# Two attention and mixture-of-experts layers: in an expert step, both transposes between gate/up and the down product

## The reference

```
x = x + L0_xattn(norm(x), ctx)          # 16 heads of 16 channels, cross attention
x = x + L0_ffn(norm(x))                 # 16 experts, 4 a token, chosen by groups; a shared expert
x = x + L1_xattn(norm(x), ctx, mask)    # the same with biases and a mask
x = x + L1_ffn(norm(x))                 # 16 experts, 2 a token; a shared expert
```

## Time and profile before

| what | value |
|---|---|
| time, median of 3 (lowest, highest) | 2484.33 us (2482.01, 2484.53) |
| the profiled execution's own time | 2487.88 us |
| its span | 2486.0 us |
| TensorE busy, matmuls | 2044.5 us (82%) |
| TensorE busy, weight loads | 1599.3 us (64%) |
| VectorE, ScalarE, GpSimd busy | 59%, 43%, 45% |
| granted TensorE clock, mean | 0.931 |
| expert phases | about 774 to 1257 us and 2041 to 2287 us |

### The profile page before, as it was taken

The page is one execution under the profiler, slowest core; times in us unless marked ns, Lnnn a source line. Parts: engine busy times, 40 slices in busy tenths (PEclk is TensorE's granted clock), DMA queues, the critical chain, the costliest instruction groups (busy, mean ns, idle before and its releaser), DMA issues.

```text
span 2486.0 us, 52846 instructions
## 1 busy us (share of the span) xinstructions
PE 2044.5 (82%) x16352; PEld 1599.3 (64%) x16353; DVE 1467.8 (59%) x4591; ACT 1068.5 (43%) x2276; POOL 1121.9 (45%) x1595
## 2 busy tenths in 40 slices
PE   4999999999965999999948989889998849997000
PEld 3777777777754878777736766666666637786000
DVE  3677777777762444444436877777777624443333
ACT  2555555555522333333325555555555513332000
POOL 1455555555556000000056777777777341001676
PEclk8999999999987999999969999999999969999555
DMA  5222222222226444444434333333333154444555
GB/s 204 58 79 80 79 80 80 82 82 78 76 83 148 150 146 150 151 146 151 149 123 171 102 101 101 103 101 107 98 102 101 41 105 150 150 149 132 177 175 169
DMA packets 206442, 292.77 MB, mean 118 GB/s; under 512 B 34230, under 2 KB 155320, under 8 KB 205880
## 3 DMA queue, kind: packets, MB, share of 16 engines
q1 hardware_dynamic: 164199, 185.12, 22.9%
q0 software_dynamic: 37584, 102.81, 13.2%
q10 hardware_dynamic: 4608, 4.20, 1.3%
HBM read 155.69 MB, written 136.33 MB: 117 GB/s over the span
## 4 chain that ended last, share of the span: by engine, by line
PE 59%; POOL 18%; issue 12%; DVE 4%; DMA 4%; ACT 2%; SPq 1%; POOLq 1%; DVEq 0%; ACTq 0%
PE ps L1435 16%; POOL ygath L615 10%; PE ps L1443 7%; PE ps L1371 5%; POOL xsort L559 4%; PE ps L1448 4%; PE ps L1309 3%; PE ps L1287 3%; PE ps L1321 3%; PE ps L1263 3%; PE ps L1346 2%; PE ps L1380 2%; PE ps L1454 2%; POOL rstd L631 2%; PE ps L1230 2%
## 5 line engine op out<-in xcount | busy, mean ns | idle before, releaser
L1435 PE MATMUL ps<-wgu,ygath 128*128 x1664 | 441.3, 388 | 27.6 <-issue 23.0
L559 POOL DMA_INDIRECT xsort<-xn,xidx x384 | 386.7, 1007 | 134.7 <-issue 133.4
L615 POOL DMA_INDIRECT ygath<-ysort,yidx x384 | 372.5, 970 | 152.1 <-issue 99.1
L928 DVE TENSOR_REDUCE mx<-ps 128x16 f32<-128x1920 f32 x128 | 276.2, 2158 | 191.1 <-PE ps L1287 190.8
L1175 DVE TENSOR_TENSOR ygath<-ygath,ps 128x128 f32<-128x128 f32 x416 | 119.7, 288 | 442.8 <-ACT ygath L842 442.8
L1435 PEld LDWEIGHTS ps<-wgu,ygath 128*128 128x128 f32 x1664 | 285.3, 191 | 73.8 <-issue 51.6
L607 POOL CAST yidx<-rows_of 128x8 uint32 (+1 forms) x64 | 12.9, 201 | 682.2 <-SPq L297 680.4
L1371 PE MATMUL ps<-W,wsgu 128*128 128x256 f32 x1024 | 253.3, 391 | 13.7 <-ACT rt L789 12.9
L846 ACT ACTIVATE ygath<-ps 128x256 f32<-128x256 f32 x416 | 159.8, 384 | 231.4 <-PE ps L1448 231.2
L1443 PE MATMUL ps<-wd,ygath 128*128 x832 | 248.1, 380 | 2.8 <-DVE ygath L1187 2.8
L842 ACT ACTIVATE ygath<-ps 128x128 f32<-128x128 f32 x416 | 115.5, 278 | 301.4 <-PE ps L1435 301.3
(11 more groups left out here) (174 smaller groups left out, 3836.2 us busy)
## 6 DMA issues: line engine op xcount, KB each, us to landing
ygath<-xsort SPq DMA_DIRECT2D x416, 128.0 KB, 2.1
ysort<-ygath SPq DMA_DIRECT2D x208, 256.0 KB, 2.3
based<-XO SPq DMA_DIRECT2D x64, 256.0 KB, 2.3
XB<-in_x SPq DMA_DIRECT2D x32, 256.0 KB
wgu<-in_wgu SPq DMA_DIRECT2D x2, 4096.0 KB, 13.7
XB<-based SPq DMA_DIRECT2D x32, 256.0 KB
X<-based SPq DMA_DIRECT2D x32, 256.0 KB
out_x<-X SPq DMA_DIRECT2D x32, 256.0 KB, 2.3
```

Of the source, the lines that this page charges most:

```text
L559: e.indirect_dma_start(out=xsort, in_=xn2[s][:, t, :], in_offset=None, out_offset=bass.IndirectOffsetOnAxis(ap=xidx[s][:, t * 4 + k:t * 4 ...
L615: e.indirect_dma_start(out=ygath[s][:, t * 4 + k, :], out_offset=None, in_=ysort, in_offset=bass.IndirectOffsetOnAxis(ap=yidx[s][:, t * 4 ...
L928: e.tensor_reduce(mx[:, r].rearrange("p j t h -> p j (t h)"), ps[:, 4 * s:4 * s + 4, 0:4 * LK].rearrange("p j (x k) -> p j x k", k=LK), AX ...
L1435: mm = e.matmul(ps[:, 2 + h, 0:2 * F], xtT[h][:, c, :], wgu[:, bass.ds(x * (DC * 2 * F) + c * 2 * F, 2 * F)], start=(c == 0), stop=(c == D ...
```

## The change

In TensorE's step the block of the down product moves from the second place to the last. The order becomes gate and up, transpose of x, transpose of h, down product. No other engine's program changes, and no wait, buffer or operand.

```diff
                         mm.then_inc(eGU[h], 1)
-                    if not (edge and n < 4):
-                        _, h, k = tile(4, r, w, c2)
-                        x = tile_experts[1][r]
-                        e.wait_ge(eHT[h], k)
-                        e.matmul(ps[:, 6 + h, 0:D], hT[h], wd[:, bass.ds(x * D, D)],
-                                 start=True, stop=True).then_inc(eD[h], 1)
                     if not (edge and n >= NT[L]):
                         e.wait_ge(xl[r], 16 * w + 16)
                         for c in range(DC):
...
                         e.wait_ge(eH[h], k)
                         e.transpose(ps[:, 4 + h, 0:P], hm[h], ident).then_inc(eHT_ps[h], 1)
+                    if not (edge and n < 4):
+                        _, h, k = tile(4, r, w, c2)
+                        x = tile_experts[1][r]
+                        e.wait_ge(eHT[h], k)
+                        e.matmul(ps[:, 6 + h, 0:D], hT[h], wd[:, bass.ds(x * D, D)],
+                                 start=True, stop=True).then_inc(eD[h], 1)
```

## The result

| kernel | median (lowest to highest) | runs | profiled span | turn of the loop |
|---|---|---|---|---|
| before | 2484.40 us (2482.01 to 2484.53) | 4 | 2486.0 us | 14.08 us |
| after | 2510.45 us (2507.63 to 2514.89) | 4 | 2510.9 us | 14.63 us |

The change makes the kernel slower: the ratio is 1.0109, 95% interval 1.009 to 1.0127. Predicted were 2514 us, a turn of 14.67 us and 0.90 for slower.

The account below looks back on a forecast made before the run. TensorE was taken as full in mid-loop steps, losing 1.08 us a turn at two register loads. 13.5 us (top) + 16.5 us (early load) = 30 us on 2484.33 gave 2514 us, range 2504 to 2528.

Parts of the forecast that it names:

- A full step: Mid-loop expert step, matmul behind matmul without gap: stays 1.62 us after the reorder, cost zero.
- The ring: Cycle through TensorE and VectorE in each step: 1.50 us a round, 1.59 in step 0 of four, fitting within 1.62.
- the tight ring: The 1.59 us round in step 0 of four: if 0.1 too long, up to 10 us over 104 steps.
- theory H: Both gaps of a turn are set by VectorE's hT copy ending, as the down product's register instruction holds TensorE's sequencer.
- the sharp form of H: Only a waiting control instruction holds TensorE's sequencer; without it no gaps, turn 13.0 to 13.1 us, 2430 us.
- The top, 0.26 us: Register load at the loop's top: hT copy ends 0.26 us later, gap grows equally; 52 x 0.26 = 13.5 us.
- static instructions: Ten the sequencer passes behind line 1443's register instruction; six moved ahead of the wait may give back up to 0.08 us.
- The early load: Register load behind step 1 of a turn's first group of four: gap grows 0.33 us; 50 x 0.33 = 16.5 us.
- The sum, 30 us: Whole kernel: 13.5 us at the loop's top plus 16.5 us at the early load makes it 30 us slower.
- The step on the queue: TensorE's queue rule would hide the wait at no cost; set aside because a control instruction waits; no-change chance 0.06.

Follow-up runs that it names:

- e3: Kernel after, but with the down product between the transpose of x and the transpose of h; VectorE unchanged: 2503.26 us, turn 14.46 us.
- e1: Kernel after, but VectorE copies hT ahead of the down product's copy: 2443.54 us, turn 13.40 us.
- e2: Kernel before, TensorE's old order kept, but VectorE copies hT ahead of the down product's copy: 2473.44 us, turn 13.90 us.
- e5: Kernel after, with TensorE's early register load moved from behind step 1's down product to ahead of it: 2481.11 us, turn 14.00 us.
- e6: e1 with the register load of the loop's top issued four steps earlier, only unpacking left at the top: 2431.58 us, turn 13.09 us.
- e7: Kernel after, VectorE's order kept, with the register load of the loop's top issued four steps earlier: 2503.27 us, turn 14.45 us.
- e4: Kernel after, with expert 0's down weights fixed for all tiles, so the down product has no register instruction: 2500.82 us, turn 14.42 us.

## Why the prediction was right

**A full step costs nothing: right.** 1.62 us with no piece between the blocks. The ring of down product, down copy, hT copy and next down product fits: the down product follows in its slot, and in the 880 to 1200 us of the kernel after nothing waits for line 1187 on TensorE; over the whole run it is 2.4 us in 4 waits, before 2.8 in 4. The 10 us of reserve for the tight ring weren't needed.

**The gaps hang on the end of the hT copy: shown.** Moved later by less (e3), moved earlier (e1, e2), and with the work behind it moved ahead (e5, e6), the turn follows each time: within 0.1 us of what theory H gave in all but e7, where I had priced one gap too high. The exception is the sharp form of H, that only a waiting register instruction holds the sequencer: e4 took 14.42 us a turn for its 13.0 to 13.1.

**The top, 0.26 us: the hT copy moved as forecast, the gap a little less.** The copy ends 886.45 - 885.49 = 0.96 us ahead of the point where the array runs dry, before 898.77 - 897.55 = 1.22 us: 0.26 later. The sequencer's chain from there shrank from 1.68 to 1.63 us, so the gap grew by 0.21 (0.46 to 0.67). The prediction had allowed up to 0.08 for static instructions that no longer stand behind the wait; whether these 0.05 are that, the rows of the sequencer, which give tenths, don't show. The early load speaks against it: the same six instructions moved ahead of the wait there, and its chain stayed at 1.30 us.

**The early load, 0.33 us: exact** (a gap of 0.10 became 0.43, with the chain behind the copy at 1.30 us both times).

**The sum, 30 us: 26 measured.** 52 x 0.21 + 50 x 0.33 = 27.4 by the profiled gaps; the top's 0.05 is 2.6 us of the difference. The expert phases of the profiled executions grew by 28.1 us. Outside them the kernel after took 1755.7 us and the kernel before 1758.9; over all nine profiles that part lies between 1751.1 and 1758.9 us, although no run changes it, so I take these 3.2 us for scatter. With scatter of that size the total is a loose test of the forecast; the two gaps and the turn are the closer one.

**The step on the queue: right result, wrong reason.** The Trainium skill (Advanced Engine Details and Errata, section Sequencer Loop) has engine instructions wait in a queue while the sequencer reads on. I set it aside because the instruction that waits here is a control instruction. e4 took that away, and the time stayed: a weight load with an unmet wait held TensorE's sequencer as well. The measurement decides here. It is made on the weight load of the down product alone; no run here tries another engine instruction.

## What to carry to other kernels

When an engine is full in its steady state, look for the places where its sequencer has something slow to do (a loop's end, a register load), and ask which wait is the last one ahead of it; the gap is that release plus the chain behind it, less the time for which the engine still has work. Moving a matmul to a later place costs the full engine nothing by itself, but it can delay the release of such a wait: here the moved matmul's copy stood in VectorE's order ahead of the copy that everything waited for. Change the order on both engines together (e1), and put slow register work behind the earliest release (e6).

## What the runs showed that I had not expected

An unmet wait in the down product's weight load stops TensorE's sequencer as a wait in a register instruction does (e4: 898.28 to 898.3). The loop's closing instruction on TensorE takes 207 to 215 ns in the rows above, on ScalarE 45 (by line, kernel e4).

A gate-and-up block behind a gap takes 1.12 or 1.13 us for 0.86, so each gap costs 0.26 us beside its own length, however short it is: 0.10 us of gap before, 0.67 after. The chain need not show a piece for it: the top's block in e7 takes 1.11 us and one in e2 takes 1.12 with none ahead. Only when the load is covered further does it shrink, to 0.95 at the early load of e6. Closing the last 0.13 us of the top's gap therefore saved 0.13 + 0.26 = 0.39 us a turn, of which the 0.09 at the early load took some back: 0.30. The block of e2, in its chain:

```profile
902.44 0.11 PE ps L1454
902.55 1.12 PE ps L1435 x4
```

The two closings, by line, kernel e4:

```profile
L355 PEldq COMPARE_BRANCH  x1: 208/208/208, 898.4 to 898.4; - x1
...
L355 ACTq COMPARE_BRANCH  x1: 45/45/45, 898.8 to 898.8; - x1
```
